# A five-part transformer block on one core: periods written out without loops, constants and statistics moved in the start, and an order of their own for each attention's first periods

## The chip, the cores and the metric

The kernel runs on one core of a Trainium2 chip. Its engines are TensorE (PE; its weight loads are PEld), VectorE (DVE), ScalarE (ACT), GpSimd (POOL) and SyncE (SP), which issues most DMAs. The metric is the time of one execution in microseconds (us): 991.41 before, the median of three runs (989.72 to 997.21). The profiled execution took 990.86, of which the span of its instructions is 989.1.

## What is computed

Eight batches of 56 tokens of width 128 (x) pass through four layers. L0 is a modulated cross attention with 16 heads of 8 onto a context of 1500 rows per batch; L1 is a one-head attention onto the same context with gated experts; L2 and L3 are blocks of self attention, cross attention onto the context with 16 heads, and an MLP. All in float32.

```python
xq = _ada_ln(x_q, t_vec, Wss_q, bss_q)           # L0
xkv = _ada_ln(x_kv, t_vec, Wss_kv, bss_kv)
q = (xq @ Wq + bq).reshape(B, Lq, nh, dh)
kv = (xkv @ Wkv + bkv).reshape(B, Lkv, 2, nh, dh)
scores = jnp.einsum('bqhd,bkhd->bhqk', q, k) / jnp.sqrt(jnp.float32(dh))
attn = jax.nn.softmax(scores, axis=-1)
...
q_c = _ln(x) @ W_qc + b_qc                       # L2, after its self attention
kv_c = _ln(context) @ W_kvc + b_kvc
...
kv = (context @ kv_w + kv_b).reshape(B, S, 2, H, HD)   # L3
```

## The kernel before

The three cross attentions with 16 heads (L0, L2, L3; class `Heads`) are most of the time. A context of 1500 rows is taken in three parts of 500 (j = 0 to 2), each of four pieces of 125 rows. For one batch the steps are, with the names used below:

- context work, by `deps`, `dpow`, `norm`, `hat` on POOL (L0 and L2 only): normalised rows `hat_sb`; T0 to T2: their transposes on PE (L511) and ACT's copies (L612, L616); K0 to K2: key products (L519), which ACT reads twice (L630) and POOL cuts into three bfloat16 parts (L753 to L760); V0 to V2: value products (L526), copied by ACT (L636). SP then stacks the key parts in `kstack` by 18 small DMAs (L364), six for each j. The queries are cut and stacked likewise in `qstack` (six DMAs, L355).
- maxima: 24 products M0.0 to M2.7 (L542, part j and pair of heads), each read by a DVE reduction (L675); then MTa and MTb, transposes of the maxima (L532), called MT below, whose result goes into `qstack` as a shift by DVE and ACT.
- scores S0 to S11 (L556, eight products each), exponentials E0 to E11 on ACT (L648), products with the values PV0 to PV5 (L568), then OT and OTT, which finish a batch.

All T, K, V, M, MT, OT and OTT share three PSUM banks (`ring_ps`). A bank is written again only when its last reader is done, and which bank a step has follows from the order written out (`ring_banks`). The period of batch n holds the scores of batch n, the maxima of batch n+1 and the context work of batch n+2, interleaved in an order written by hand (`pe`, `act`). `first_context` does the context work of batch 0 alone; the fill (period -1) has the maxima of batch 0 and the context work of batch 1, in an order `fill` on PE. `later_periods` (L187) emits the fill, period 0, a hardware loop of two turns with two periods each (periods 1 to 4), and periods 5 to 7 written out. In the loop, addresses and the values waited for are registers; `settle` adds a semaphore increment before some steps.

At the start, POOL clears one of two key stacks (L1466), and ACT clears the other and writes its two rows of ones (L1615) after the context work of batch 0. DVE takes the statistics of the eight contexts for L0 and L2 (L1686, L1690: 12 + 12 instructions each): batch 0 to 4 before the maxima, 5 to 7 in one block behind the fill (`after_first`). Twelve modulation products for the layers L2 and L3 (L1499, MODS_LATER) stand between K and V of batch 0. L1's attention is the class `Evidence`. `keep_busy` issues products whose result nobody reads. The own (self) attentions of L2 and L3 (class `Own`) run beside the context work of batch 0 of their cross attention: its V products stand just ahead of the own scores (L886).

## Time and profile before

| engine | busy us of 989.1 | share |
|---|---|---|
| PE | 868.6 | 88% |
| DVE | 606.3 | 61% |
| ACT | 507.4 | 51% |
| POOL | 361.6 | 37% |

The chain of work that ended last is 62% PE, 18% DVE, 9% issue, 5% ACT. The slices of 24.7 us show PE at 5, 7, 6, 6 tenths in the first 100 us and at 9 in the middle of each attention. In the rows below a group gives the busy time of the engines in a window with the number of instructions, the granted clock of PE (1.00 is 2.4 GHz, 0.50 is 1.2 GHz), the DMA engines' busy share and GB/s; or the instructions in order of time with what ended the idle time before them.

### The profile page before, as it was taken

The page shows a single profiled execution, that of the slowest core. Times are in us where ns is not written, and L with a number is a line of the kernel's source. Part 1 is how long each engine was busy: PE and PEld are TensorE (multiplying, and loading weights), DVE is VectorE, ACT ScalarE, POOL GpSimd, SP SyncE. Part 2 cuts the span into 40 slices and gives each one's busy share as a digit, 9 for nine tenths or more (in the row PEclk, how much of TensorE's full clock was granted, in tenths as well). Part 3 has the DMA queues.
Part 4 walks back from the last instruction along what each step waited for, and adds up shares of the span by engine and source line. Part 5 has one row for each costly group of instructions (what it writes and reads, how often), then busy time and mean ns, then how long its engine had stood idle before and what let it go on. Part 6 is the DMA issues. An engine that isn't in the chain of part 4 may idle for free.

```text
span 989.1 us, 24937 instructions
## 1 busy us (share of the span) xinstructions
PE 868.6 (88%) x9539; PEld 556.6 (56%) x9539; DVE 606.3 (61%) x1273; ACT 507.4 (51%) x754; POOL 361.6 (37%) x481
## 2 busy tenths in 40 slices
PE   5766999999898887778999999888787999999987
PEld 3434777776555434542777777554453466666653
DVE  7557777777332374555677777715464777777825
ACT  5565777775512213312777777441333466667551
POOL 6645666661000106147566664010313333333000
PEclk9677999999989999886999999999789799999999
DMA  9742444437326304307244443010334444443200
GB/s 264 201 112 77 126 127 125 124 95 257 109 114 188 94 0 132 99 16 197 74 122 132 124 125 98 19 63 1 87 94 125 120 126 126 126 124 95 64 2 9
DMA packets 76826, 106.67 MB, mean 108 GB/s; under 512 B 9371, under 2 KB 70427, under 8 KB 76481
## 3 DMA queue, kind: packets, MB, share of 16 engines
q1 hardware_dynamic: 75152, 102.65, 37.4%
q10 hardware_dynamic: 1584, 2.79, 1.0%
q8 instruction: 62, 1.02, 0.4%
q14 instruction: 28, 0.22, 0.1%
HBM read 41.56 MB, written 0.23 MB: 42 GB/s over the span
## 4 chain that ended last, share of the span: by engine, by line
PE 62%; DVE 18%; issue 9%; ACT 5%; POOL 3%; DMA 2%; SPq 1%; ACTq 0%; POOLq 0%; DVEq 0%
PE ring_ps L542 11%; PE oacc_ps L568 11%; PE score_ps L556 10%; PE ring_ps L526 7%; PE ring_ps L519 6%; DVE max_sb L675 4%; PE ring_ps L1174 4%; DVE tok L961 3%; PE ring_ps L532 2%; PE ring_ps L511 2%; PE oacc_ps L334 2%; ACT prob_sb L648 1%; POOL hat_sb L744 1%; DMA prob_sb<-ctx_T 1%; DVE bn_tmp L1686 1%
## 5 line engine op out<-in xcount | busy, mean ns | idle before, releaser
L675 DVE TENSOR_REDUCE max_sb<-ring_ps 128x1 f32<-128x500 f32 x576 | 364.0, 674 | 151.1 <-PE ring_ps L542 150.2
L648 ACT ACTIVATE prob_sb<-score_ps 125x896 f32<-125x896 f32 x288 | 255.1, 919 | 88.0 <-PE score_ps L556 87.0
L542 PE MATMUL ring_ps<-kstack,qstack 128*128 128x500 bf16 x576 | 201.1, 393 | 14.7 <-DVE max_sb L675 8.6
L753 POOL TENSOR_TENSOR key_sb<-key_sb,part_sb 128x500 f32<-128x500 f32 x72 | 81.8, 1136 | 236.8 <-ACT key_sb L630 236.8
L556 PEld LDWEIGHTS score_ps<-qstack,kstack 128*128 128x128 bf16 (+1 forms) x2304 | 138.3, 102 | 48.8 <-ACT prob_sb L648 13.1
L556 PE MATMUL score_ps<-qstack,kstack 128*128 128x112 bf16 (+3 forms) x2304 | 160.5, 214 | 5.9 <-ACT prob_sb L648 5.0
L568 PE MATMUL oacc_ps<-prob_sb,val_sb 125*32 125x168 f32 (+1 forms) x3456 | 139.5, 294 | 1.5 <-ACT prob_sb L648 1.4
L568 PEld LDWEIGHTS oacc_ps<-prob_sb,val_sb 125*32 125x32 f32 x3456 | 97.6, 109 | 48.8 <-issue 19.1
L542 PEld LDWEIGHTS ring_ps<-kstack,qstack 128*128 128x128 bf16 (+1 forms) x576 | 51.3, 98 | 87.7 <-issue 53.8
L744 POOL TENSOR_SCALAR hat_sb<-nat_sb,norm_now 125x128 f32<-125x128 f32 x192 | 87.2, 471 | 4.9 <-POOL norm_now L734 4.9
L760 POOL TENSOR_TENSOR part_sb<-key_sb,part_sb 128x500 bf16<-128x500 f32 x72 | 82.0, 1138 | 5.8
L1218 POOL TENSOR_TENSOR tok_rstd<-tok_var,minus_half 112x4 f32<-112x4 f32 x8 | 8.1, 1008 | 207.5 <-DVE tok_var L1232 207.5
L334 PE MATMUL oacc_ps<-ident,mean_mat 128*128 128x512 bf16 x272 | 72.7, 406 | 0.0
L636 ACT COPY val_sb<-ring_ps 125x384 f32<-125x384 f32 x72 | 34.6, 480 | 54.3 <-PE ring_ps L526 54.3
L519 PE MATMUL ring_ps<-ctxT_sb,w_sb 128*128 128x500 f32 x96 | 55.0, 666 | 5.8 <-ACT key_sb L630 5.8
L526 PE MATMUL ring_ps<-w_sb,ctxT_sb 128*125 128x128 f32 x384 | 55.6, 293 | 3.3 <-ACT val_sb L637 2.9
L630 ACT ACTIVATE part_sb<-ring_ps,vec_sb 128x500 bf16<-128x500 f32 x72 | 48.9, 679 | 17.8 <-PE ring_ps L519 14.2
L1252 ACT COPY qpart_sb<-prob_sb 64x448 bf16<-64x448 bf16 x30 | 16.9, 562 | 80.1 <-DVE prob_sb L1241 79.3
L526 PEld LDWEIGHTS ring_ps<-w_sb,ctxT_sb 128*125 128x125 f32 x384 | 52.9, 206 | 6.7 <-ACT val_sb L637 4.1
L1174 PE MATMUL ring_ps<-tok,w_sb 128*128 128x448 f32 x98 | 43.9, 584 | 10.5 <-DVE part_sb L1809 3.6
L511 PE MATMUL ring_ps<-ident,hat_sb 125*128 125x125 f32 x192 | 32.7, 299 | 23.2 <-DVE max_sb L675 8.6
L630 ACT ACTIVATE key_sb<-ring_ps,vec_sb 128x500 f32<-128x500 f32 x72 | 48.6, 675 | 0.0
(217 smaller groups left out, 993.6 us busy)
## 6 DMA issues: line engine op xcount, KB each, us to landing
kstack<-part_sb SPq DMA_DIRECT2D x432, 125.0 KB, 2.4
...
qstack<-qpart_sb SPq DMA_DIRECT2D x24, 224.0 KB, 3.6
...
```

The costliest lines, as they stand in the source:

```text
L334: pe.matmul(out.rearrange("p (a k) -> p a k", a=2), busy_lhs, busy_rhs, start=True, stop=True)
L519: last = pe.matmul(ps[:, 0:KB], self.wkey, self.context_T(u)[:, j * KB:(j + 1) * KB], start=True, stop=True)
L526: last = pe.matmul(ps[0:CK, c * D:(c + 1) * D], self.context_T(u)[:, k0:k0 + CK], self.wval, start=True, stop=True)
L542: last = pe.matmul(ps[:, 0:KB], queries(p, n, D), kstack[:, u, p, j * KB:(j + 1) * KB], start=True, stop=True)
L556: last = pe.matmul(score_ps[0:window(c), c % 2, p // 4, at:at + 2 * LQ], kstack[:, u, p, c * CK:c * CK + window(c)], queries(p, n), start= ...
L568: return pe.matmul(oacc_ps[tile * GW:(tile + 1) * GW, at:at + nh * LQ], val_sb[0:CK, u, c, g * GW:(g + 1) * GW], prob_sb[0:CK, c % PROBS, ...
L630: ins = act.activation(dst, src, ACT.Identity, bias=self.bkey)
L648: ins = act.activation(dst, score_ps[0:CK, c % 2, :, 0:HALF], ACT.Exp)
L675: ins = dve.tensor_reduce(max_sb[:, p, j:j + 1], ring_ps[:, self.bank[name], 0:KB], AX.X, ALU.max)
L744: ins = pool.tensor_scalar(hat_sb[:, c, :], nat_sb[0:CK, u, c, :], norm_now[:, 1, c:c + 1], norm_now[:, 0, c:c + 1], ALU.add, ALU.mult)
L760: ins = pool.tensor_tensor(part_sb[:, 2, cols], rest, part_sb[:, 1, cols], ALU.subtract)
L1174: last = pe.matmul(self.ps(name) if out is None else out, lhsT, rhs, start=(k == 0), stop=(k == len(pairs) - 1))
```

## The change

- The loops of `later_periods` and of SP's `sync_later` are written out; no registers are left in them. `settle` is gone.
- `fill` is gone. A table for each attention gives the place of the context steps on PE and ACT in its first periods (`EARLY_L0`, `EARLY_L2`, `EARLY_L3`: period -1 and 0, in L0 also 1); "K1:M0.2" puts K1 behind M0.2, "-" puts a step first. Banks follow from these orders, and `first_context` has banks of its own.
- POOL clears both key stacks at the beginning; ACT writes both pairs of rows of ones before its first copy. The queries' six DMAs go from ACT's queue to SP's, the first five ahead of the keys'.
- DVE takes the statistics of batches 1 to 4 before the maxima, and those of 5, 6 and 7 in periods 0, 1 and 2, one instruction behind each of the 24 maxima.
- The later modulations move into Evidence, on PE behind its first scores in the place of seven of ten filler products, on DVE behind the first maximum.

```diff
-def later_periods(body, eng, after_first=None):
+def later_periods(body):
 
     body(None, None, (0, 0, 0), (1, 1, 0))
-    if after_first:
-        after_first()
     body(None, (0, 0, 0), (1, 1, 0), (2, 0, 1))
-    with eng.Fori(0, (B - 4) // 2) as j:
-        body((2 * j, 0, j), (2 * j + 1, 1, j), (2 * j + 2, 0, j + 1), (2 * j + 3, 1, j + 1))
-        body((2 * j + 1, 1, j), (2 * j + 2, 0, j + 1), (2 * j + 3, 1, j + 1), (2 * j + 4, 0, j + 2))
+    for n in range(B - 4):
+        body(*((k, k % 2, k // 2) for k in range(n, n + 4)))
...
-                if modulated:
-                    fill = [*mm[0:8], "T0", *mm[8:10], "T1", *mm[10:12], "T2", "K0", *mm[12:16], "K1", *mm[16:20], "K2",
-                            *mm[20:24], "V0", "V1", "MTa", "MTb", "V2"]
-                else:
-                    fill = [*T3, "K0", "K1", "K2", "V0", "V1", *mm, "MTa", "MTb", "V2"]
-                self.fill = fill
...
+                def moved(eng, n):
+
+                    order, after = self.orders[eng], dict(x.split(":") for x in early[n][eng].split())
+                    fixed = [x for x in order if not context(eng, x) and (n >= 0 or lead(x) == 1)]
+                    return [y for x in ["-", *fixed] for y in ([x] if x != "-" else []) + [z for z in after if after[z] == x]]
+
+                self.early = {(eng, n): moved(eng, n) for n in early for eng in ("pe", "act")}
...
-                self.fill_bank = {**self.steady_bank, **ring_banks(fill)}
+                self.early_bank = {n: {**self.steady_bank, **ring_banks(self.early["pe", n])} for n in early}
+                self.first_bank = ring_banks([n for n in pe if context("pe", n)])
...
                 first = not nxt and far
-                filling = nxt and not cur and not prev
-                self.bank = self.fill_bank if filling else self.steady_bank
+                n = cur[0] if cur else -1 if nxt else B
+                self.bank = self.first_bank if first else self.early_bank.get(n, self.steady_bank)
...
-                for name in self.fill if filling and eng == "pe" else self.orders[eng]:
+                for name in self.early.get((eng, n), self.orders[eng]):
...
-                        settle(pe)
...
-                    keep_busy(pe, 2 if k else 10, ring_ps[:, 0, :])
+                    if k:
+                        keep_busy(pe, 2, ring_ps[:, 0, :])
+                    else:
+                        meanwhile()
+                        keep_busy(pe, 3, ring_ps[:, 0, :])
...
                 highest(0)
+                meanwhile()
                 inverse(0)
...
+        EARLY_L0 = {
+            -1: {"pe": "T0:M1.2 T1:M1.6 T2:M2.0 K0:M2.3 K1:M2.7 K2:M2.7 V0:MTb V1:MTb V2:MTb",
...
+            1: {"pe": "T0:S0 T1:M0.2 T2:M0.5 K0:M0.5 K1:S4 K2:M1.2 V0:M2.5 V1:M2.5 V2:MTb",
...
+            stack_queries(sp, queries_ready(d0), a0.qstacked, (0, 1))
             sp.wait_ge(keys_cleared, 1)
-            a0.sync_batch(sp, None, (0, 0, 0))
+            a0.sync_batch(sp, None, (0, 0, 0), lambda: stack_queries(sp, queries_ready(d0), a0.qstacked, (2,)))
...
-            sp.wait_ge(keys_cleared, 3)
+            sp.wait_ge(keys_cleared, 2)
...
-            pool.memset(kstack[:, 0, :, :].bitcast(F32), 0.0).then_inc(buffers_ready, 1)
-            pool.wait_ge(buffers_ready, 1)
+            for u in range(2):
+                pool.memset(kstack[:, u, :, :].bitcast(F32), 0.0).then_inc(buffers_ready, 1)
+            pool.wait_ge(buffers_ready, 2)
...
-            pe.wait_ge(loaded_wm, 16)
-            d.bank_free(pe, "mods1")
-            modulations(MODS_LATER, "mods1")
...
+            def later_modulations():
+                pe.wait_ge(d1.dve.sem, d1.dve.after("anchors"))
+                pe.wait_ge(loaded_wm, 16)
+                modulations(MODS_LATER, "mods1")
+
+            evi.tensor(pe, lambda eng: eng.wait_ge(d1.dve.sem, d1.dve.after("qk")), later_modulations)
...
-            act.wait_ge(buffers_ready, 1)
-            fill(key_stack(0)[SHIFT_ROW:SHIFT_ROW + 2, :], bf16_ones[:, :], 1.0).then_inc(keys_cleared, 1)
+            for u in range(2):
+                act.wait_ge(buffers_ready, u + 1)
+                fill(key_stack(u)[SHIFT_ROW:SHIFT_ROW + 2, :], bf16_ones[:, :], 1.0).then_inc(keys_cleared, 1)
             act.wait_ge(d.dve.sem, d.dve.after("scales0"))
             act.wait_ge(values_cleared, VALUES)
-            a0.first_context("act", act, 0)
             act.wait_ge(queries_cleared, 2)
-            for j in range(NJ):
-                a0.first_part("act", act, lambda name, j=j: name in (f"k0.{j}", f"K{j}"))
-                d.to_blocks(act, (j,))
-                stack_queries(act, queries_ready(d), a0.qstacked, (j,))
+            a0.first_part("act", act, lambda name: name in ("T0", "T1"), starts=True)
+            d.to_blocks(act, (0,))
+            a0.first_part("act", act, lambda name: name == "T2")
+            d.to_blocks(act, (1,))
+            a0.first_part("act", act, lambda name: name in ("k0.0", "K0"))
+            d.to_blocks(act, (2,))
+            a0.first_part("act", act, lambda name: name[0] in "kK" and name[-1] != "0")
             a0.first_context("act", act, 2)
-            fill(key_stack(1), mean_mat[:, 0:1], 0.0).then_inc(keys_cleared, 1)
-            act.wait_ge(keys_cleared, 2)
-            fill(key_stack(1)[SHIFT_ROW:SHIFT_ROW + 2, :], bf16_ones[:, :], 1.0).then_inc(keys_cleared, 1)
...
-            def statistics(n):
+            def statistics(n, steps=range(2 * NC)):
...
+            def later_statistics(name, cur):
+
+                if cur and cur[0] + STATS_FIRST < B and name in a0.mm:
+                    statistics(cur[0] + STATS_FIRST, (a0.mm.index(name),))
...
-            for n in (1, 2, 3):
+            for n in range(1, STATS_FIRST):
                 statistics(n)
-            modulations(MODS_LATER, SCALES_LATER, 1)
-            statistics(4)
-            a0.later("dve", dve, lambda: [statistics(n) for n in (5, 6, 7)])
+            a0.later("dve", dve, beside=later_statistics)
...
-            evi.vector(dve)
+            evi.vector(dve, lambda: modulations(MODS_LATER, SCALES_LATER, 1))
```

The order tables have 14 such strings in all; two are shown.

On PE from the key products of batch 0 into the fill stands before (L519 is K, L1499 a modulation product, L526 V, L542 M, L511 T):

```order
L519 MATMUL ring_ps<-ctxT_sb,w_sb 128x500 x3
L1499 MATMUL score_ps<-cond_silu,w_sb 128x8 x12
L526 MATMUL ring_ps<-w_sb,ctxT_sb 125x128 x12
L542 MATMUL ring_ps<-kstack,qstack 128x500 x8
L511 MATMUL ring_ps<-ident,hat_sb 128x125 x4
L542 MATMUL ring_ps<-kstack,qstack 128x500 x2
L511 MATMUL ring_ps<-ident,hat_sb 128x125 x4
L542 MATMUL ring_ps<-kstack,qstack 128x500 x2
L511 MATMUL ring_ps<-ident,hat_sb 128x125 x4
L519 MATMUL ring_ps<-ctxT_sb,w_sb 128x500
L542 MATMUL ring_ps<-kstack,qstack 128x500 x4
L519 MATMUL ring_ps<-ctxT_sb,w_sb 128x500
```

and now, with the same steps at other line numbers (L504 is K, L511 V, L527 M, L496 T):

```order
L504 MATMUL ring_ps<-ctxT_sb,w_sb 128x500 x3
L511 MATMUL ring_ps<-w_sb,ctxT_sb 125x128 x12
L527 MATMUL ring_ps<-kstack,qstack 128x500 x11
L496 MATMUL ring_ps<-ident,hat_sb 128x125 x4
L527 MATMUL ring_ps<-kstack,qstack 128x500 x4
L496 MATMUL ring_ps<-ident,hat_sb 128x125 x4
L527 MATMUL ring_ps<-kstack,qstack 128x500 x2
L496 MATMUL ring_ps<-ident,hat_sb 128x125 x4
L527 MATMUL ring_ps<-kstack,qstack 128x500 x3
L504 MATMUL ring_ps<-ctxT_sb,w_sb 128x500
L527 MATMUL ring_ps<-kstack,qstack 128x500 x4
L504 MATMUL ring_ps<-ctxT_sb,w_sb 128x500 x2
```

The modulation products are gone, and T and K come later among the M. Behind these rows stand before: four M, K2, four M, V0 and V1 of batch 1, MT, V2; now: MT and then V0 to V2.

On DVE from the fill's maxima into period 0 stands before (L1686 and L1690 are statistics, L675 the read of a maximum, L691 the shift):

```order
L675 TENSOR_REDUCE max_sb<-ring_ps 128x1 x24
L678 TENSOR_REDUCE max<-max_sb 128x8
L682 TENSOR_SCALAR maxb<-max 128x8
L685 CAST maxparts<-maxb 128x8
L687 SCALAR_TENSOR_TENSOR maxparts<-max,maxb 128x8
L691 CAST qstack<-ring_ps 2x4x112
L1686 BN_STATS bn_tmp<-w_sb 125x6 x12
L1690 BN_AGGR ctx_mv<-bn_tmp 125x2 x12
L1686 BN_STATS bn_tmp<-tok 125x6 x12
L1690 BN_AGGR ctx_mv<-bn_tmp 125x2 x12
L1686 BN_STATS bn_tmp<-w_sb 125x6 x12
L1690 BN_AGGR ctx_mv<-bn_tmp 125x2 x12
```

and now (L1710, L1712, L656, L672):

```order
L656 TENSOR_REDUCE max_sb<-ring_ps 128x1 x24
L659 TENSOR_REDUCE max<-max_sb 128x8
L663 TENSOR_SCALAR maxb<-max 128x8
L666 CAST maxparts<-maxb 128x8
L668 SCALAR_TENSOR_TENSOR maxparts<-max,maxb 128x8
L672 CAST qstack<-ring_ps 2x4x112
L656 TENSOR_REDUCE max_sb<-ring_ps 128x1
L1710 BN_STATS bn_tmp<-w_sb 125x6
L656 TENSOR_REDUCE max_sb<-ring_ps 128x1
L1710 BN_STATS bn_tmp<-w_sb 125x6
```

The block of three behind the fill's maxima has become single instructions between the maxima of a period.

On PE the head of the loop's first period (M0.0, OT, S0) is before

```order
L542 ISA
L542 MATMUL ring_ps<-kstack,qstack 128x500
L177 ISA x2
L586 MATMUL ring_ps<-ident,o_sb 56x128 x3
L589 MATMUL ring_ps<-fold_sb,o_sb 56x64 x2
L177 ISA x2
L556 ISA
L556 MATMUL score_ps<-qstack,kstack 128x112
L556 ISA
L556 MATMUL score_ps<-qstack,kstack 128x112
L556 ISA
L556 MATMUL score_ps<-qstack,kstack 128x112
```

and the head of period 1 now is, up to T0 of batch 3 and M0.1

```order
L527 MATMUL ring_ps<-kstack,qstack 128x500
L570 MATMUL ring_ps<-ident,o_sb 56x128 x3
L573 MATMUL ring_ps<-fold_sb,o_sb 56x64 x2
L541 MATMUL score_ps<-qstack,kstack 128x112 x8
L496 MATMUL ring_ps<-ident,hat_sb 128x125 x4
L527 MATMUL ring_ps<-kstack,qstack 128x500
```

Each of the eight products of S0 had an instruction ahead of it that sets a register for its address; now there is none.

## Rows read from the trace of the kernel before

**Rows 1.** Windows, cut from one MT's start to another's (columns: busy us and count)

```profile
105.91:205.90 99.99, 99.94 (x1293) 70.74 (x1289) 72.17 (x140) 74.23 (x112) 65.79 (x98) 1.00 0.46 124
205.90:230.41 24.51, 24.51 (x326) 17.52 (x322) 17.76 (x35) 18.48 (x28) 11.40 (x15) 1.00 0.32 87
495.10:594.02 98.92, 98.88 (x1293) 70.27 (x1290) 72.12 (x140) 72.59 (x112) 65.80 (x98) 1.00 0.46 126
594.02:618.36 24.34, 24.34 (x326) 17.48 (x323) 17.77 (x35) 17.98 (x28) 10.49 (x14) 1.00 0.36 96
801.06:898.60 97.54, 96.75 (x1244) 65.13 (x1241) 69.95 (x140) 65.28 (x100) 34.19 (x36) 1.00 0.45 127
898.60:922.01 23.41, 23.37 (x315) 15.96 (x311) 17.57 (x35) 16.23 (x25) 8.56 (x9) 1.00 0.37 101
```

**Rows 2.** Windows of the start, a clock drop, and L2's fill (columns as above)

```profile
0.00:100.00 100.00, 65.11 (x388) 41.48 (x389) 65.35 (x260) 54.27 (x62) 57.65 (x86) 0.80 0.61 164
20.00:45.00 25.00, 17.64 (x63) 13.06 (x62) 14.48 (x99) 9.75 (x19) 18.17 (x28) 0.61 0.98 246
278.00:280.00 2.00, 2.00 (x13) 2.00 (x13) 0.16 (x1) 0.00 (x0) 1.01 (x1) 0.58 0.03 8
460.00:472.00 12.00, 9.87 (x25) 2.95 (x25) 10.26 (x21) 0.21 (x1) 7.72 (x15) 0.50 0.44 119
```

**Rows 3.** Timeline of PE at the start (start, us, idle before in brackets)

```profile
32.15 5.13 PE L1499 MATMUL score_ps<-cond_silu,w_sb 128*128 128x8 f32 x24
...
44.59 1.91 PE L542 MATMUL ring_ps<-kstack,qstack 128*128 128x500 bf16 x4
...
56.74 1.06 PE L511 MATMUL ring_ps<-ident,hat_sb 125*128 125x125 f32 x4 [6.12 <-ACT ctxT_sb L612]
...
83.29 1.07 PE L511 MATMUL ring_ps<-ident,hat_sb 125*128 125x125 f32 x4 [8.42 <-DVE max_sb L675]
```

**Rows 4.** Timeline of ACT at the start

```profile
18.41 0.77 ACT L612 ACTIVATE ctxT_sb<-ring_ps,mod_sb 128x500 f32<-128x500 f32 x1 [4.85 <-PE ring_ps L511]
...
45.51 5.20 ACT L1615 ACTIVATE kstack<-mean_mat 128x6000 f32<-128x6000 f32 x1
```

**Rows 5.** Timeline of DVE, the last of three statistics

```profile
79.23 2.42 DVE L1686 BATCH_NORM_STATS2 bn_tmp<-w_sb 125x6 f32<-125x128 f32 x12
81.68 0.90 DVE L1690 BATCH_NORM_AGGREGATE ctx_mv<-bn_tmp 125x2 f32<-125x6 f32 x12
```

**Rows 6.** Timeline of PE, S0 of L3: first loop period, then period 5

```profile
802.88 1.18 PE L556 MATMUL score_ps<-qstack,kstack 128*128 x8
...
900.52 0.55 PE L556 MATMUL score_ps<-qstack,kstack 128*128 128x112 bf16 x8
```

**Rows 7.** Timeline of POOL at the start

```profile
1.24 5.10 POOL L1466 MEMSET kstack<- 128x6000 f32 x1
...
14.93 7.00 POOL L744 TENSOR_SCALAR hat_sb<-nat_sb,norm_now 125x128 f32<-125x128 f32 x12 [0.25 <-POOL norm_now L734]
...
39.95 5.16 POOL L744 TENSOR_SCALAR hat_sb<-nat_sb,norm_now 125x128 f32<-125x128 f32 x12 [0.24 <-POOL norm_now L734]
```

**Rows 8.** DMA issues from 20 to 48 us (count, KB each, us to landing)

```profile
kstack<-part_sb SPq DMA_DIRECT2D x18, 125.0 KB, 4.1
qstack<-qpart_sb ACTq DMA_DIRECT2D x6, 224.0 KB, 4.9
```

**Rows 9.** Timelines of L2: PE (V1, S0), SP (queries), DVE (maxima)

```profile
402.35 2.07 PE L526 MATMUL ring_ps<-w_sb,ctxT_sb 128*125 128x128 f32 x8 [0.74 <-ACT val_sb L637]
...
442.48 3.79 SPq L355 DMA_DIRECT2D qstack<-qpart_sb  x6
...
454.84 14.22 DVE L675 TENSOR_REDUCE max_sb<-ring_ps 128x1 f32<-128x500 f32 x24 [11.51 <-PE ring_ps L542]
...
473.25 0.56 PE L556 MATMUL score_ps<-qstack,kstack 128*128 128x112 bf16 x8
```

**Rows 10.** Timeline of PE in Evidence, first transposes

```profile
294.12 1.57 PE L1045 MATMUL ring_ps<-ident,key_sb 128*125 128x128 f32 x12 [1.27 <-ACT key_sb L1074]
```

More of the change, by code:

```diff
@@ L793, in load_T, with sync_batch @@
                 sp.dma_start(self.context_T(u), ctx_T[n]).then_inc(self.loaded[u], 16)
-            def sync_batch(self, sp, before, this):
+            def sync_batch(self, sp, before, this, beside=None):
                 n, u, half = this
@@ L811, in sync_batch @@
                         stack_keys(sp, part_sb, part, u, slice(j * KB, (j + 1) * KB), self.stacked[u][j])
+                        if beside and j == 0 and part == 0:
+                            beside()
             def sync_load(self, sp):
@@ L1335, in project, with mods_out @@
             return product
+        def mods_out(step):
+            return d0.ps(step) if step == "mods0" else score_ps[:, 1, 1, :]
         def own_pe(d, pe, l, x_ready):
```

86 lines of the change are left out of this document (40 added, 46 removed), and 12 rows, old and new, of tables (EARLY_L0, EARLY_L2, EARLY_L3).

## The prediction

> **What bounds the kernel now.** I read the windows of the periods first. From one MT (transposes of the maxima) to the next TensorE (PE) is busy all the time at full clock: 24.51 of 24.51 us in period 5 of L0 [rows 1]. Such a period is bound by PE. In the first 100 us it is busy 65.1 us only, at a granted clock of 0.80, and from 20 to 45 us the DMA engines are 0.98 busy at 246 GB/s [rows 2]. So the start is bound by something else, and the timelines there name it. The first M (product for the maxima) starts only at 44.59, behind the later modulations (5.13) and the V products in PE's order [rows 3]. Then ScalarE (ACT) runs two fills of the second key stack, the first at 45.51 for 5.20, the other behind it, and PE waits 6.12 for ACT's copy of a transpose [rows 3, 4]. Then VectorE (DVE) runs the statistics of three contexts, up to 82.5, and PE waits 8.42 for a ring bank that DVE must read first [rows 3, 5].
>
> Then the pace of the middle, again by windows cut at the starts of MT: the loop's four periods take 99.99 us in L0, 98.92 in L2 and 97.54 in L3, so 25.00, 24.73 and 24.39 each; period 5, the same work written out, takes 24.51, 24.34 and 23.41 [rows 1]. The difference sits where each of the eight products of S0 has a register instruction ahead of it in the loop: S0 lasts 1.18 in a loop period of L3 and 0.55 written out [rows 6].
>
> **The start of L0.** All against the profiled execution: span 989.1, time 990.86; the median of the runs, 991.41, is 0.5 above.
> POOL's second clearing of key rows (the first took 5.10 from 1.24 [rows 7]) ends at 11.44, and the power that makes the deviations, at 10.95 before, comes 0.5 late with all behind it. ACT's second row of ones (5.2) goes behind the first, to 18.8; the first T copy stood at 18.41 after a wait of 4.85 [rows 4], which hides the fill. Without that cover it costs 5.2. The two key fills at 45.5 are gone from ACT.
> POOL's first hats took 7.00, beside DVE's casts on SBUF, later ones 5.16 [rows 7]. At that ratio the second clearing takes 6.9 and the start is 2.3 late instead of 0.5. I take 0.5, since DVE mostly runs statistics there, and keep 2.3 as the bound. A rule speaks for the bound: the Trainium skill (GPSIMD Engine Reference, section Key points) says that GpSimd shares its SBUF interfaces with VectorE and contends with some of its instructions. By it the sum would be 1.8 higher; the trace agrees with it on the hats.
> With the modulations gone, K2 and the V products not waiting for a bank, ACT is done with the keys at about 30 and PE with V at about 33. M0.0 needs the stacked queries and the first third of the stacked keys. In 20 to 45 us DMA moved 246 x 25 = 6.15 MB [rows 2], of which queries are 1.38, keys 2.30 [rows 8] and the last context 0.77, so 1.7 MB of loads lie ahead of them; queries and a third of the keys are in after (1.70 + 1.38 + 0.77) / 0.246 = 15.7 us, at 35.7. That the queries now go through SP's queue, behind the context loads, is in this sum. DVE does four statistics of 3.4 in a row behind its query split and is free at 35.2. So M begins at about 35.5, 9.1 earlier.
> 24 maxima take DVE 14.2 [rows 9], to 50.1. T0 to T2 of batch 1 sit at M1.2 to M2.0, about 42 to 47, and POOL's hats can be ready from 40.5 to 44: no wait. K1 and K2 come behind M2.7, MT at about 52, then all three V, so S0 at 56.5. Bounds: 55 at full clock, 60 if PE stays at half clock as it did in L2's fill (0.50 in 460 to 472 [rows 2]).
> Period 0: in L2, which has no statistics, S0 to MT is 495.10 - 473.25 = 21.85 [rows 1, 9]. The statistics become 24 pieces in each of three periods, 2.42 + 0.90 = 3.3 us [rows 5]. DVE is busy 18.0 in a loop period [rows 1] and stays under PE with 21.3, but the first half is tight: I take 0.7 for each of the three, between 0 (all in gaps) and 3.3 (all paid). MT behind period 0 comes at 56.5 + 21.85 + 0.7 + 0.5 (clearing) = 79.5 instead of 105.91: **-26.4**.
> Period 1: POOL cuts batch 2's keys until about 79.3, needs 2.8 for the deviations and 1.7 for a first hat, to 83.8, while PE reaches T0 behind S0 at about 82.2: **+1.6** (0 to 4). The statistics of periods 1 and 2 add 1.4, and T1 and T2 asked for later give back 0.7: **+0.7**.
>
> **The loops.** Four periods each at the written-out pace: 99.99 - 98.04 = 1.95 in L0, 98.92 - 97.36 = 1.56 in L2, 97.54 - 93.64 = 3.90 in L3 [rows 1]: **-7.4**. Registers of the other engines go too, but hide behind PE.
>
> **L2.** In the own attention V1 and V2 now have a bank free: two waits of 0.74 for ACT go [rows 9], ahead of the first own scores: **-1.5** (0 if something else is late there). In the fill M starts at 450 instead of 454.4, since the last of six query DMAs is issued by 446.3 [rows 9] and the products ahead of it are fewer; but K1, K2 and V stand between the M. PE at half clock then needs 24 x 0.42 + 9.2 = 19.3, to 469.4, and DVE was done at 469.1: no gain. At full clock DVE's 14.2 plus 2 ends at 466.3. I take 1.2. V2 no longer stands between MT and S0: 0.8. **-2.0** (-5 to +0.5).
> **L3.** One such wait goes in the own part, **-0.7**. In the fill the first M waits for the query DMAs, which nothing moves; V products moved into it and V2 taken out cancel: 0 (-2 to +1.5).
>
> **The later modulations** now run beside Evidence: 5.13 at half clock [rows 3], so 2.6 at full, in the place of seven filler products. PE stood there filling from 290.5, and waited 1.27 for ACT's exponential until 294.12 [rows 10]: 290.5 + 2.6 + 0.7 for three fillers = 293.8, hidden, and DVE's two small steps too. What can come is the clock: it fell to 0.58 in 278 to 280 [rows 2], where PE ran the 8-column anchor products, and these have that form. At half clock for some 6 us, 3 are lost, and U0 behind them releases DMAs of the chain. I take **+1.0** (0 to 3.3).
>
> Sum: -26.4 + 1.6 + 0.7 - 7.4 - 1.5 - 2.0 - 0.7 + 1.0 = -34.7. 990.86 - 34.7 = **956.2**.
>
> **Rivals.**
> 1. The start gives a good part back: statistics fully paid (3 x 3.3 less the 2.1 counted, +7.8), fill at half clock (+3.5), clearing late (+1.8), hats late (+2.4), together 15.5: 971.7. For it: PE and DVE are both near full in those periods. Against: three ring banks absorb pieces of 0.2.
> 2. DMA bounds the start, and M0.0 comes no earlier than 44. Then PE still saves the 6.12 and the 8.42: 990.86 - 14.5 - 7.4 - 3.2 = 965.8. For it: the 0.98. Against: the bytes above.
> 3. The edit does not do what it says: each wait is followed by the next one (hat, stack, bank). The loops alone: 983.5, within 1%.
> 4. Slower: PE's stream is longer, and fetching it stalls in the twelve periods newly written out. It decides from 34.7 / 12 = 2.9 us each; at 4 us 990.86 - 34.7 + 48 = 1004.2. Against it: period 5 is such code and runs with PE busy throughout [rows 1].
> The Trainium skill (Runtime: NRT & Kernel Launch, Instruction fetch mechanics) says that the sequencer streams straight code ahead and that a taken branch breaks this; by it rival 4 has next to no chance, and the trace agrees on straight code. The 0.03 below does not rest on it.
>
> **How the numbers follow.** Forecast (944 to 966) 0.77; rivals 1 and 2 (966 to 981) 0.15; rival 3 0.05; rival 4 0.03. Range 944 to 972: the low end is the sum with hats and statistics free (-4), the L2 fill at full clock (-3), no clock loss (-1) and 4 more of PE's idle time in the first 100 us; the high end takes in rival 1 whole. One per cent, 9.9 us, is about what a measurement here can tell from no change. Faster 0.92, same 0.05, slower 0.03.
>
> **What would show it.** After: first M at 35 to 36, MT at 52 and 79.5; no ACT fill behind 19; periods 2 to 4 at 24.5, 24.3 and 23.4; small pieces on DVE between the maxima of periods 0 to 2, and no PE wait over 1 us there; own scores of L2 1.5 closer to V0; clock 1.00 beside Evidence. A first M behind 40, PE waiting over 2 us for DVE in one of the periods 0 to 2, or written-out periods over 25 would make it wrong.

## The result and the profile after

The changed kernel takes 963.46 us (median of four runs, 960.46 to 968.04) against 990.98 before in the same comparison: a ratio of 0.971 with the interval 0.966 to 0.976, so 27.5 us faster where 34.7 had been forecast. The profiled execution took 962.78, with a span of 961.0; before the span was 989.1. What follows sets the marks of this execution against those of the profiled execution before; a mark is the start of a step on PE.

The page's slices of 24 us (tenths of busy time, and of the granted clock) show the start filled up: PE reads 6 5 8 9 in the first four slices, 5 7 6 6 before:

```profile
PE   6589999998997897877999999888686899999986
...
PEclk9699999999899998878999999999887799999999
```

Windows of the changed kernel: from S0 to the MT behind period 0 of L0, its period 1, periods 2 to 4, period 5 (compare [rows 1]); then S0 to MT and periods 1 to 4 of L2; then M0.0 to the fill's MT, S0 to MT, and periods 1 to 4 of L3. Columns as in [rows 1]: start and end, length, then the busy time and count of PE, of its weight loads, of DVE, ACT and POOL, then the granted clock, the DMA share and GB/s.

```profile
62.16:86.08 23.92, 22.45 (x299) 15.04 (x298) 18.95 (x52) 18.05 (x27) 19.15 (x28) 1.00 0.52 139
86.08:112.00 25.92, 25.09 (x322) 17.34 (x322) 20.90 (x59) 18.33 (x28) 21.37 (x35) 1.00 0.52 138
112.00:185.53 73.53, 73.53 (x967) 52.55 (x968) 56.85 (x129) 55.18 (x84) 48.87 (x73) 1.00 0.46 125
185.53:209.95 24.42, 24.42 (x326) 17.53 (x322) 17.77 (x35) 18.39 (x28) 11.13 (x14) 1.00 0.36 96
446.00:468.85 22.85, 22.84 (x298) 16.51 (x299) 15.91 (x28) 16.88 (x25) 14.49 (x20) 0.93 0.32 87
468.85:566.34 97.49, 97.49 (x1292) 69.92 (x1288) 72.16 (x140) 72.16 (x112) 65.91 (x98) 1.00 0.47 127
...
732.92:751.31 18.39, 13.35 (x49) 5.68 (x49) 15.18 (x28) 1.94 (x6) 4.49 (x5) 0.78 0.83 185
753.93:777.87 23.94, 23.53 (x287) 15.16 (x287) 15.71 (x28) 15.29 (x22) 8.56 (x9) 0.88 0.31 82
777.87:870.82 92.95, 92.83 (x1244) 63.87 (x1240) 70.31 (x140) 64.80 (x100) 34.24 (x36) 1.00 0.47 134
```

The written-out periods run at the pace of period 5, as forecast. What was not forecast stands in the last three rows: the fill of L3 takes 18.39 (15.4 before), and period 0 of L3 runs at a clock of 0.88, for 23.94 (21.2 before).

The account of the whole, from one mark of PE to the next (us, negative is faster):

| stretch | forecast | measured |
|---|---|---|
| start of L0 to the MT behind period 0 | -26.4 | -19.8 |
| period 1 of L0 (hats, pieces, loop) | +1.8 | +0.9 |
| rest of L0 | -1.5 | -1.5 |
| L0's last MT to the own scores of L2 | -0.5 | -6.2 |
| fill and period 0 of L2 | -2.0 | +0.4 |
| periods 1 to 4 of L2 | -1.6 | -1.4 |
| L2's last MT to the own scores of L3 | -0.7 | -2.0 |
| own scores to the MT behind period 0 of L3 | 0 | +6.5 |
| periods 1 to 5 of L3 | -3.9 | -4.8 |
| behind L3 | 0 | -0.2 |
| sum | -34.7 | -28.1 |

The start, on PE (start, us, idle before in brackets): M0.0, MT and S0.

```profile
38.12 6.14 PE L527 MATMUL ring_ps<-kstack,qstack 128*128 128x500 bf16 x11 [7.29 <-DMA kstack<-part_sb]
...
57.92 1.03 PE L517 MATMUL ring_ps<-ident,maxparts 128*2 128x128 f32 x8 [1.95 <-DVE maxparts L668]
...
62.16 0.56 PE L541 MATMUL score_ps<-qstack,kstack 128*128 128x112 bf16 x8
```

M0.0 waits for a transfer, and comes 2.6 behind the 35.5 of the forecast; MT is 5.9 behind its 52, S0 5.7 behind its 56.5. The two waits of [rows 3, 4, 5], for ACT's copy and for the block of statistics, are gone. On DVE two of the five waits between the maxima, and the two small steps ahead of MT:

```profile
45.85 2.44 DVE L656 TENSOR_REDUCE max_sb<-ring_ps 128x1 f32<-128x500 f32 x4 [0.49 <-PE ring_ps L527]
48.78 1.27 DVE L656 TENSOR_REDUCE max_sb<-ring_ps 128x1 f32<-128x500 f32 x2 [0.50 <-PE ring_ps L527]
...
55.58 1.13 DVE L663 TENSOR_SCALAR maxb<-max 128x8 bf16<-128x8 f32 x1
56.74 1.05 DVE L666 CAST maxparts<-maxb 128x8 f32<-128x8 bf16 x1
```

### The profile page after: what moved, and what is told of

It reads as the page before. It is cut to its first block, busy times and chain, and to the rows that moved or that the text cites. A ratio compares the mean times of both kernels' runs of the same rounds, so it can differ in the third digit from the quotient of the medians.

```text
span 961.0 us, 22829 instructions
## 1 busy us (share of the span) xinstructions
PE 848.7 (88%) x9532; PEld 546.9 (57%) x9532; DVE 607.5 (63%) x1273; ACT 499.9 (52%) x753; POOL 366.4 (38%) x482
## 3 DMA queue, kind: packets, MB, share of 16 engines
q10 hardware_dynamic: 720, 1.41, 0.5%
## 4 chain that ended last, share of the span: by engine, by line
PE 62%; DVE 16%; issue 8%; POOL 5%; ACT 4%; DMA 3%; SPq 1%; POOLq 0%; DVEq 0%; ACTq 0%
PE ring_ps L527 13%; PE oacc_ps L553 11%; PE score_ps L541 10%; PE ring_ps L511 6%; PE ring_ps L504 6%; DVE max_sb L656 4%; PE ring_ps L1162 4%; DVE tok L944 3%; PE ring_ps L517 2%; PE ring_ps L496 2%; PE oacc_ps L320 2%; ACT prob_sb L630 1%; POOL hat_sb L722 1%; DMA prob_sb<-ctx_T 1%; POOL kstack L1482 1%
## 5 line engine op out<-in xcount | busy, mean ns | idle before, releaser
L656 DVE TENSOR_REDUCE max_sb<-ring_ps 128x1 f32<-128x500 f32 x576 | 366.6, 674 | 136.8 <-PE ring_ps L527 134.8
L527 PE MATMUL ring_ps<-kstack,qstack 128*128 128x500 bf16 x576 | 198.9, 390 | 28.3 <-DVE max_sb L656 9.0
L541 PE MATMUL score_ps<-qstack,kstack 128*128 128x112 bf16 (+1 forms) x2304 | 158.2, 215 | 6.9 <-ACT prob_sb L630 5.0
L527 PEld LDWEIGHTS ring_ps<-kstack,qstack 128*128 128x128 bf16 x576 | 50.9, 98 | 96.5 <-issue 50.1
L511 PE MATMUL ring_ps<-w_sb,ctxT_sb 128*125 128x128 f32 x384 | 49.7, 275 | 3.1 <-ACT key_sb L612 1.8
L504 PE MATMUL ring_ps<-ctxT_sb,w_sb 128*128 128x500 f32 x96 | 51.2, 627 | 0.8 <-ACT key_sb L612 0.3
L511 PEld LDWEIGHTS ring_ps<-w_sb,ctxT_sb 128*125 128x125 f32 x384 | 47.1, 188 | 6.5 <-ACT key_sb L612 2.8
L320 PEld LDWEIGHTS oacc_ps<-ident,mean_mat 128*128 128x128 bf16 x272 | 28.5, 108 | 37.0 <-issue 18.3
```

The source lines that it names most:

```text
L320: pe.matmul(out.rearrange("p (a k) -> p a k", a=2), busy_lhs, busy_rhs, start=True, stop=True)
L504: last = pe.matmul(ps[:, 0:KB], self.wkey, self.context_T(u)[:, j * KB:(j + 1) * KB], start=True, stop=True)
L511: last = pe.matmul(ps[0:CK, c * D:(c + 1) * D], self.context_T(u)[:, k0:k0 + CK], self.wval, start=True, stop=True)
L527: last = pe.matmul(ps[:, 0:KB], queries(p, n, D), kstack[:, u, p, j * KB:(j + 1) * KB], start=True, stop=True)
L541: last = pe.matmul(score_ps[0:window(c), c % 2, p // 4, at:at + 2 * LQ], kstack[:, u, p, c * CK:c * CK + window(c)], queries(p, n), start= ...
L656: ins = dve.tensor_reduce(max_sb[:, p, j:j + 1], ring_ps[:, self.bank[name], 0:KB], AX.X, ALU.max)
```

## Experiments

Each kernel was profiled once, beside timed runs of the kernel before; the marks are read from its trace. A time marked "once" is that of a single execution; one of those is no measure of a difference of a few us, and there the marks carry the reading.

### The loops alone

```diff
# the kernel before
-    with eng.Fori(0, (B - 4) // 2) as j:
-        body((2 * j, 0, j), ...)
+    for n in range(B - 4):
+        body(*((k, k % 2, k // 2) for k in range(n, n + 4)))
# the same in sync_later, and no increment in settle
```

> The kernel before with only its loops written out (periods 1 to 4 of each attention on every engine, SP's too, and the settle increments gone); nothing else is moved. Theory 1 (the pace of a written-out period is all that the loops are worth, as predicted): the four periods from MT to MT take 98.0 in L0, 97.4 in L2, 93.6 in L3 or a little less, time 983.5 (983 to 984.5), all other marks as in the kernel before, Evidence and the own attention of L2 among them. Theory 2 (the 2.0 us that the changed kernel gained inside Evidence and the 2.0 more than forecast in L2's own attention come with the straight code): the same stretches are 2 shorter here too, time 979.5. Theory 3 (straight code stalls somewhere): a period over 25.

978.74 median (975.02 to 983.88), a ratio of 0.987 (0.982 to 0.993). Periods 1 to 4 of L0, L2 and L3:

```profile
104.70:202.66 97.96, 97.96 (x1292) 70.09 (x1288) 72.28 (x140) 73.63 (x112) 65.96 (x98) 1.00 0.47 126
485.93:583.54 97.61, 97.61 (x1292) 69.87 (x1289) 72.28 (x140) 72.22 (x112) 66.15 (x98) 1.00 0.47 128
789.91:882.88 92.97, 92.86 (x1245) 63.83 (x1242) 70.32 (x140) 64.83 (x100) 34.30 (x36) 1.00 0.47 134
```

Against [rows 1] they gain 2.0, 1.3 and 4.6, together 7.9 where 7.4 was forecast; period 5 of L3, which was written out before, gains another 0.2 (23.41 to 23.23) now that settle's increments are gone. S0 lasts 0.56 to 0.57 in these periods. In the loop it took 1.00 to 1.26 in L3 [rows 6], but only 0.57 to 0.80 in L0 and L2: S0 holds about half of L3's gain of 1.14 a period and a quarter of the 0.50 and 0.33 of the other two. Where in the period the rest is gained is not shown. No period is over 25, so theory 3 is out. But the median fell by 12.6, and from L0's last MT to the own scores of L2 this kernel took 149.4 instead of 154.6, with the same instructions. Theory 2 had said something like that; the next run asks whether that stretch varies by itself.

### The kernel before, again

> The kernel before, once more, unchanged. From the last MT of L0 to the first own scores of L2 the kernel before took 154.64 in its profile; the four profiles of kernels with written-out loops show 148.41 to 149.97 there, though Evidence and the own attention are the same work in the kernel with only its loops written out. Theory 1 (that stretch varies from execution to execution with the clock's dips and DMA waits): 149 to 153 here. Theory 2 (loops or settle cost something behind the attentions too): 154 to 155 again, and the periods 25.0, 24.7 and 24.4 again.

988.2, once. The stretch took 152.4, as theory 1 has it, and the periods of the loop were 25.0, 24.8 and 24.4 again (means). The twelve kernels with written-out periods, the changed one among them, took 147.5 to 152.2 there, 149.8 in the mean; the kernel before 154.6 and 152.4. So the stretch varies by 2 between two executions of one kernel and by 4 to 5 over kernels that have nearly the same work in it, and of the 6.2 in the table 3.7 are left by the means, 1 to 2 of them for the two V waits (below). Whether straight code, or settle's going, gains the rest stays open: two profiles of the kernel before are too few to tell.

### The old fills of L2 and L3

```diff
# the changed kernel
-            -1: {"pe": "K0:- K1:- K2:- V0:M0.5 V1:M1.2 V2:M1.3",           # L3
+            -1: {"pe": "K0:- K1:- K2:- V0:- V1:- V2:MTb",
# and the like in L2: T, K, V0, V1 first, V2 behind MT
```

> The changed kernel with the fill (period -1) of L2 and of L3 in the old order: K and V0, V1 ahead of the first M, V2 behind MT; period 0 keeps its new order. The changed kernel took 18.4 from the first M to MT in L3 where the kernel before took 15.4, and PE stood idle for 6.69 ahead of the first M. Theory 1 (V products between the maxima starve DVE, and the idle PE stays at half clock into period 0): M to MT in L3 falls to 15.4, MT to S0 rises from 2.6 to 3.4, S0 to the MT behind period 0 falls from 23.9 to about 21.5, so L3 ends 4.5 earlier; in L2 S0 to MT falls from 22.85 to 21.85, its fill stays within 1. Theory 2 (the new order of period 0 itself is slower): the fills change by 2 at most and both periods 0 stay at 22.85 and 23.9, L3 ends 2 earlier.

956.59, once. M to MT and S0 to MT of L3:

```profile
731.44:746.84 15.40, 12.37 (x25) 2.37 (x26) 14.73 (x28) 0.00 (x0) 4.88 (x6) 0.56 0.78 179
...
750.20:771.41 21.21, 20.98 (x288) 13.85 (x287) 15.70 (x28) 15.70 (x24) 8.55 (x9) 0.99 0.45 129
```

Theory 1 holds to 0.3 in each of the three stretches: the fill 3.0 shorter, MT to S0 0.7 longer, period 0 2.7 shorter; L3 ends 5.0 earlier by them, where 4.5 was expected. In L2 M to MT is 15.43 and S0 to MT 21.86, with MT to S0 at 3.4, but M0.0 comes 4.2 later behind the own scores, so that the MT behind period 0 is only 1.1 earlier behind them. In the changed kernel DVE, the pace of a fill, stood idle 1.41 when V0 came between the maxima and took 2.07 at half clock:

```profile
735.07 2.50 DVE L656 TENSOR_REDUCE max_sb<-ring_ps 128x1 f32<-128x500 f32 x4 [0.17 <-PE ring_ps L527]
738.98 3.02 DVE L656 TENSOR_REDUCE max_sb<-ring_ps 128x1 f32<-128x500 f32 x5 [1.41 <-PE ring_ps L527]
```

while ahead of the maxima PE stands idle for the queries' transfers anyway, and V0 and V1 are free. The clock of the changed kernel from MT on, four us each:

```profile
751.31:755.31 4.00, 3.24 (x18) 2.17 (x19) 0.61 (x1) 0.96 (x2) 0.00 (x0) 0.50 0.00 0
755.31:759.31 4.00, 4.00 (x13) 1.73 (x13) 1.36 (x2) 2.56 (x4) 1.03 (x1) 0.50 0.00 0
```

and of this one, with V2 behind MT:

```profile
746.84:750.84 4.00, 4.00 (x25) 3.34 (x26) 0.61 (x1) 0.91 (x3) 0.00 (x0) 0.55 0.00 0
750.84:754.84 4.00, 3.80 (x33) 2.08 (x31) 2.04 (x3) 3.95 (x8) 1.49 (x2) 1.00 0.57 192
```

With V2 behind MT PE was busy for all of the first four us, and the clock was back at 1.00 behind them; with V2 moved away it took eight, and the first 5.4 us of period 0 ran at 1.2 GHz. V2 is all that differs on PE between MT and S0; the run moved V0 and V1 along with it, and none moved V2 alone.

### The steady order in periods 0 and 1

```diff
# the changed kernel: EARLY_L0[0], EARLY_L0[1], EARLY_L2[0] and EARLY_L3[0] are left out
```

> The changed kernel with the steady order of steps in period 0 (and 1) of L0, L2 and L3; only the fills keep their new orders. Theory 1 (the clock, not the order, makes period 0 of L2 and L3 long): S0 to MT stays at 22.85 in L2 and 23.9 in L3 (plus or minus 0.5), and in L0 period 0, whose T then stand ahead of POOL's hats, grows from 23.9 by up to 6 and period 1 by 2. Theory 2 (the order of period 0 is slower than the steady one): L2 and L3 fall to 21.9 and 21.2 here. If the new orders in L0 are worth nothing, its period 0 stays at 23.9.

967.6, once. S0 to MT is 22.45 in L2 and 23.62 in L3: their long period 0 is not the order's, as theory 1 says. In L0 it grew to 28.72, as theory 1 says too, but period 1, which was to grow by 2, fell to 24.60:

```profile
61.92:90.64 28.72, 23.45 (x299) 16.33 (x298) 18.95 (x52) 17.93 (x27) 23.81 (x37) 0.94 0.46 126
90.64:115.24 24.60, 24.60 (x326) 17.46 (x322) 20.78 (x59) 18.39 (x28) 16.62 (x26) 1.00 0.47 127
```

The order of period 0 that puts T behind POOL's hats is worth 4.8; 1.3 of it is given back in period 1, where POOL is behind in its turn. PE busy 24.60 of 24.60 beside the pieces of a context's statistics on DVE also says what those cost: 0.1 against the 24.46 of a period without.

### Loads behind the first keys

```diff
-            for n in range(2, 7):
+            for n in range(2, 5):
                 load_context(sp, stats_buffer(n), n, stats_loaded[n])
...
             a0.sync_batch(sp, None, (0, 0, 0), ...)
+            for n in range(5, 7):
+                load_context(sp, stats_buffer(n), n, stats_loaded[n])
```

> The changed kernel with the loads of contexts 5 and 6 (0.77 MB each) issued behind the stacking of the first keys instead of ahead of it; their statistics are taken in periods 0 and 1 only. In the changed kernel M0.0 came at 38.12, forecast was 35.5, and from 30 to 38 us DMA was 1.11 busy at 240 GB/s. Theory 1 (transfers bound the first M): it comes earlier by up to 2 x 0.77 / 0.24 = 6, cut off by DVE, whose fourth statistics end at 36.5, so at 33 to 36.5, and MT of the fill 1.6 to 2 earlier (56.2). Theory 2 (POOL's cut of the keys or the issue on SP's queue bounds it): M0.0 stays at 37.5 to 38.1.

961.29, once. PE at M0.0:

```profile
32.64 0.81 PE L527 MATMUL ring_ps<-kstack,qstack 128*128 128x500 bf16 x3 [1.30 <-DMA kstack<-part_sb]
36.43 4.70 PE L527 MATMUL ring_ps<-kstack,qstack 128*128 128x500 bf16 x8 [2.98 <-DVE max_sb L656]
```

1.54 MB fewer ahead of the keys brought M0.0 forward by 5.5, so transfers bound it. That is a little more than theory 1 had, and MT came at 54.46 where 56.2 was expected, 3.5 earlier than in the changed kernel: DVE's fourth statistics take 3 of the gain back, as the wait of 2.98 shows.

### Joined, with fewer statistics and earlier T and K

```diff
# the old fills and the late loads, all of ACT's key copies ahead of the shift, and
-        STATS_FIRST = 5
+        STATS_FIRST = 4
-            -1: {"pe": "T0:M1.2 T1:M1.6 T2:M2.0 K0:M2.3 K1:M2.7 K2:M2.7 V0:MTb ...   # L0
+            -1: {"pe": "T0:M1.2 T1:M1.5 T2:M1.7 K0:M2.0 K1:M2.2 K2:M2.5 V0:MTb ...
```

> The changed kernel with the old fills of L2 and L3, the loads of contexts 5 and 6 behind the first keys, three contexts' statistics ahead of the maxima instead of four (STATS_FIRST = 4: batch 4 in period 0 and so on), and T1, T2, K0 to K2 of L0's fill earlier (behind M1.5, M1.7, M2.0, M2.2, M2.5) with all of ACT's key copies ahead of the shift. Theory 1 (DVE's fourth statistics were what M waited for once the transfers were out of its way, and POOL's cut of the keys is what makes DVE's maxb and part0 1.1 long instead of 0.17): maxima from 33.2, MT of the fill at 51 to 52 instead of 57.92, POOL's cut ends before maxb or else maxb stays slow; MT behind period 0 at 79 to 80.5 instead of 86.08; with the 6.9 of L3 and 1.1 of L2, 949 by the profile. Theory 2 (hats and bank waits take the place): MT of period 0 at 83 or later, 953.

957.73 median (955.00 to 959.46). Maxima began at 33.19, but MT came at 54.81 and MT behind period 0 at 85.09: theory 2, though the time is above the 953 that it named. POOL's hats of batch 1 came at 38 to 43 as before (its cut of the first keys ends at 35.2, as it does with four statistics and the late loads), so T0 could start at 39.77 only, and DVE waited 1.60 there, and 1.18 more behind the K. POOL's cut then ran beside the end of the maxima. DVE, and POOL in the same stretch:

```profile
53.16 0.43 DVE L663 TENSOR_SCALAR maxb<-max 128x8 bf16<-128x8 f32 x1
53.63 1.05 DVE L666 CAST maxparts<-maxb 128x8 f32<-128x8 bf16 x1
```

```profile
52.44 1.13 POOL L737 TENSOR_TENSOR part_sb<-key_sb,part_sb 128x500 bf16<-128x500 f32 x1
53.53 1.13 POOL L731 TENSOR_TENSOR key_sb<-key_sb,part_sb 128x500 f32<-128x500 f32 x1
```

Each of the two small steps ends within 0.03 of the end of a POOL instruction. In the changed kernel they took 1.13 and 1.05 in the same way, from 55.58; in L2, where POOL makes no keys then, 0.17 each. S0 then stood 6.36 behind MT instead of 4.24, at a clock of 0.73.

### The statistics in a block again

```diff
-            a0.later("dve", dve, beside=later_statistics)
+            a0.later("dve", dve, beside=block)       # 5, 6, 7 behind the fill's shift
```

> The changed kernel with the statistics of 5, 6 and 7 in one block behind the fill's shift again, not spread. Theory 1 (as predicted, PE waits for the block): DVE is busy with it for 10.2 from 59.2, PE waits 4 to 7 for a ring bank in period 0, MT behind it comes at 90 to 93 instead of 86.08, and periods 1 and 2 get 0.7 shorter each (spread pieces cost about 0.7 a period). Theory 2 (pieces cost all their time, 3.3 a period): period 0 grows by 4 and periods 1 and 2 fall by 1 and more. Theory 3 (the statistics were not the bound of period 0, POOL's hats are): MT stays within 1 of 86.08.

971.14, once. On PE:

```profile
70.26 1.01 PE L527 MATMUL ring_ps<-kstack,qstack 128*128 128x500 bf16 x2 [5.68 <-DVE max_sb L656]
```

S0 to MT grew from 23.92 to 31.19. MT came at 93.64, 7.6 later, a little past the range of theory 1. But periods 1 and 2 fell by 0.19 and 0.12 only, not 0.7 each: the pieces are nearly free, and theory 2 is out; so is theory 3.

### The modulations back at the start

```diff
# PE: between K and V of batch 0; DVE: ahead of the fourth statistics; ten fillers in Evidence
-            modulations(MODS_LATER, "mods1")          # in Evidence
+            modulations(MODS_LATER, "mods1")          # behind first_context("pe", pe, 1)
```

> The changed kernel with the later modulations back between K and V of batch 0, and ten fillers in Evidence. Theory 1 (transfers bound M0.0 of the changed kernel, so the modulations' going away was not what brought it forward): M0.0 stays at 38.1 to 38.6 and the time within 1 of the changed kernel. Theory 2 (as predicted, M0.0 comes earlier as they go): M0.0 at 40 to 44, DVE's fourth statistics later too. In Evidence, theory 1: from its first scores to the first transposes 6.3 in either; a clock cost would show as a shorter stretch here.

967.21, once; but the marks that the edit can reach moved little. M0.0 came at 39.26 (38.12 to 39.11 in the five kernels with this start), MT at 58.36 (57.60 to 58.21), L0's last MT at 233.44 (232.63 to 233.07 in three of them). So their place at the start is worth under 1 once transfers bound M0.0. The single time is 3.8 above the changed kernel's median, not within 1 as theory 1 has it, and most of that stands behind L0, in stretches that vary between the kernels: 151.4 instead of 148.4 up to the own scores of L2, and 22.17 instead of 20.52 in L2's fill. In Evidence first scores to first transposes took 6.3 here, in the changed kernel and before, and the clock was 1.00 beside the modulations in the changed kernel: no clock cost.

### The clearing back on ACT

```diff
-            for u in range(2):
-                pool.memset(kstack[:, u, :, :].bitcast(F32), 0.0).then_inc(buffers_ready, 1)
+            pool.memset(kstack[:, 0, :, :].bitcast(F32), 0.0).then_inc(buffers_ready, 1)
...
             a0.first_context("act", act, 2)
+            fill(key_stack(1), mean_mat[:, 0:1], 0.0) ...
+            fill(key_stack(1)[SHIFT_ROW:SHIFT_ROW + 2, :], bf16_ones[:, :], 1.0) ...
```

> The changed kernel with the clearing as in the kernel before: POOL clears one key stack, ACT clears the other and writes its ones (2 x 5.2) behind the V copies of batch 0. In the changed kernel ACT is idle from 31.5 to 45.4 and its first copy comes at 19.97 instead of 18.41. Theory 1 (once V and the queries no longer hold ACT back, the fills lie in that idle time): first copy at 18.4 to 18.7, fills from 31 to 41.5, no wait of PE for ACT, MT of the fill at 57.9 or up to 1 earlier. Theory 2 (the fills are on the path as they were before, where PE waited 6.12 for ACT): MT of the fill 3 to 6 later, at 61 to 64.

963.19, once. ACT, and PE at M0.0:

```profile
31.77 5.21 ACT L1633 ACTIVATE kstack<-mean_mat 128x6000 f32<-128x6000 f32 x1
37.02 5.20 ACT L1633 ACTIVATE kstack<-bf_ones 2x6000 f32<-2x6000 f32 x1
47.12 0.77 ACT L594 ACTIVATE ctxT_sb<-ring_ps,mod_sb 128x500 f32<-128x500 f32 x1 [4.90 <-PE ring_ps L496]
```

```profile
39.81 6.14 PE L527 MATMUL ring_ps<-kstack,qstack 128*128 128x500 bf16 x11 [8.60 <-DMA kstack<-part_sb]
```

The fills lie in ACT's idle time with 4.9 to spare, and the first copy came at 18.38, as theory 1 says. PE's wait of 6.12 for ACT did not come back: what took the fills off the path is that V and the queries no longer hold ACT back. But MT came at 59.30, behind a later M0.0, and so between the theories and 1.1 behind the latest of the others. S0 stood 5.59 behind it instead of 4.24:

```profile
59.30:64.89 5.59, 5.51 (x33) 4.75 (x34) 0.61 (x1) 2.95 (x8) 4.04 (x5) 0.69 0.69 195
```

L0 ended 2.8 later than in the changed kernel. Two kernels that leave the clearing on POOL show such a clock there too (0.73 in the joined one, 0.71 in the one with the old fills and the late loads), so it need not be the clearing's; one execution does not tell. Moving the clearing is thus worth between nothing and 2.8, and not the 6.12.

### Fillers ahead of the first M of L3

```diff
+                if eng == "pe" and n == -1 and not first and not self.hat:
+                    keep_busy(engine, 16)
```

> The changed kernel with 16 filler products on PE ahead of the first M of L3's fill, where it stood idle for 6.69; the V products stay among the maxima. Theory 1 (V products among the maxima are dear because PE is at half clock there): M to MT in L3 falls from 18.4 to 16.5, S0 to MT from 23.9 to 21.2. Theory 2 (they are dear in themselves, by the ring banks that they take from the maxima, and the clock falls again while DVE paces the fill): M to MT 17.5 or more, S0 to MT 23 or more. The first M itself moves by 0 to 1.

962.5, once. They stood ahead of the K products, at full clock, and left PE idle for 2.92 behind K instead of 6.69. M to MT stayed at 18.39 and S0 to MT at 23.97, the numbers of theory 2. V0 took 2.07 all the same:

```profile
732.60 0.99 PE L529 MATMUL ring_ps<-kstack,qstack 128*128 128x500 bf16 x2 [2.92 <-issue]
...
736.13 2.07 PE L513 MATMUL ring_ps<-w_sb,nat_sb 128*125 128x128 f32 x8
```

So the fillers did not bring full speed to V0, and the run leaves open whether V among the maxima is dear by the half clock or by the ring banks that it takes.

### The old fills and the late loads

```diff
# the two edits above together, no other
```

> The changed kernel with the old fills of L2 and L3 and the loads of contexts 5 and 6 behind the first keys; all else as in the changed kernel. Theory 1 (what the single profiles showed adds up): L0 3.5 shorter, L3 6.9, L2 1.1: 952 from the median of 963.5; reckoned from the joined kernel (957.7, with L0's last MT at 232.22 where the late loads alone gave 229.47) 955. Theory 2 (an earlier attention's gain is lost in the stretches between attentions): 957 to 960.

956.98 median (956.02 to 958.66), a ratio of 0.964 (0.962 to 0.967): between the two theories, and no lower than the one time of the old fills alone (956.59). L2 and L3 kept their gains. In L0 MT came at 55.22, and S0 only 5.86 behind it, where the same instructions took 4.23 in the run with the late loads alone, at a clock of 0.71 instead of 1.00. With MT 0.8 later that made L0 end at 231.87 instead of 229.47: 2.4 between two executions of the same code.

### A filler behind every M of a fill

```diff
# the kernel of the last run, and in run():
                         emit(name, batches[self.lead(name)], prev, cur, nxt)
+                        if eng == "pe" and n == -1 and not first and name in self.mm:
+                            keep_busy(engine, 1)
```

> The changed kernel with the old fills of L2 and L3 and the late loads (as in e9_best, 956.98 median), and one filler product (512 columns, 0.21 at full clock, 0.43 at half) behind each of the 24 M of every fill. The sequence that DVE paces (0.59 an M) then holds 0.43 of PE's time an M at full clock, 0.85 at half. Theory 1 (PE's idle time in the fill is what lets its clock fall to 0.50 there and stay there into the steps behind MT): the clock is 1.00 in most of the fill, MT lasts 1.03 instead of 1.87, MT to S0 falls from 3.4 to 2.3 in L2 and L3, first M to MT is 15.4 to 16.7; the time 953 to 957. Theory 2 (the clock stays at half whatever stands between the M): M to MT 20 or more in L2 and L3, the time 967 or more.

953.37 median (949.95 to 953.95), a ratio of 0.960 (0.955 to 0.966); its slowest run is 2.1 below the fastest of the kernel without the fillers, and the medians differ by 3.6. The two profiles are no measure of that difference: the one is of its kernel's fastest execution, the other of its kernel's slowest. M to MT and MT to S0 of L2 without the fillers, then with them, then of L3 with them:

```profile
429.07:444.47 15.40, 12.24 (x25) 2.42 (x25) 14.73 (x28) 0.41 (x2) 13.59 (x22) 0.59 0.65 177
444.47:448.25 3.78, 3.78 (x17) 2.84 (x18) 0.61 (x1) 0.70 (x2) 0.00 (x0) 0.50 0.00 0
```

```profile
421.93:437.34 15.41, 13.23 (x49) 3.09 (x50) 14.75 (x28) 0.48 (x2) 12.54 (x21) 1.00 0.60 165
437.34:439.29 1.95, 1.95 (x17) 1.65 (x18) 0.61 (x1) 0.53 (x2) 0.00 (x0) 1.00 0.00 0
725.16:740.56 15.40, 13.18 (x48) 3.09 (x48) 14.74 (x28) 0.00 (x0) 4.56 (x5) 1.00 0.80 171
740.56:743.81 3.25, 3.25 (x16) 2.67 (x17) 0.61 (x1) 0.52 (x1) 0.00 (x0) 0.52 0.00 0
```

The fillers cost nothing in these fills, and the clock is 1.00 through both. In L2 it stays so into S0, which comes 1.8 earlier behind MT than without. In L3 it is at 0.52 again behind MT, and 0.1 is gained. PE waits for DVE ahead of MT in both, 1.77 in L2 and 1.78 in L3, so that wait alone does not say why; the cause stays open. In L0's fill the clock was 0.80 (0.77 without), and M0.0 to MT took 20.99, where the two kernels without fillers and with the late loads took 21.82 and 22.28. So about 1.8 of the 3.6 has its place in L2, some 1 may stand in L0, and the rest is not placed. This is the fastest of the kernels.

## Why the prediction was right, and where it was off

The direction and the range held, and 27.5 came where 34.7 was forecast. The terms are further apart than the sum: the start gave 6.6 less, L2's fill and period 0 2.4 less and L3's 6.5 less, while 5.7 came from L0's last MT to the own scores of L2 that no step foresaw, part of it the variation of that stretch. That the sum came within 7 is to that extent luck. By its own steps:

- **The loops** (-7.4): 7.9 alone. Right in size, and in place only in part: S0 with its registers holds about half of the difference in L3 and a quarter in L0 and L2. No period stalled, so rival 4 is out.
- **First M at 35.5**: 38.12. The step said that queries and a third of the keys are in at 35.7 by the bytes; their transfers are the bound, as it said, but bytes by the mean rate came 2.4 short, and the late loads show that each context ahead of them costs 2.7. Rival 2 named this bound; its 44 was too late.
- **Maxima in 14.2, MT at 52**: this step failed most. From M0.0 to MT the sum had 16.5, the trace 19.8. Left out were the waits of DVE where T and K stand between the maxima (1.9 in five waits; the mean clock from M0.0 to MT was 0.70, and what the half clock has in them is not told apart) and the small steps beside POOL's cut (1.8). POOL against DVE was weighed, but for the hats and at the wrong place.
- **Period 0 at 21.85 + 0.7 + 0.5**: S0 to MT 23.92. The spread statistics cost 0.1 a period, not 0.7, and were worth 7.3 against the block; the new order of its steps, behind POOL's hats, is worth 4.8 against the steady one.
- **Period 1, +1.6 and +0.7**: hats cost 1.3, pieces 0.1. The mechanism was right, the pieces too dear.
- **The clearing (0.5) and ACT's fills**: POOL began the power at 11.44, as forecast, but ACT's first copy came at 19.97, 1.6 later than before; M0.0, which waits for a transfer, hid it. The forecast gave the end of PE's wait for ACT to the fills' going. With them put back the wait stays away: it went with the earlier V and queries.
- **The modulations** (9.1 of the earlier M partly theirs; +1.0 in Evidence): under 1 at the start, 0 in Evidence.
- **L2's own V waits** (-1.5): gone, as in the profile; from the first own products to the own scores 15.2 fell to 11.2. The kernels with both waits took 15.2, 12.4 (the kernel before, again) and 13.0 (the loops alone), so 1 to 2 is theirs. The rest of the 6.2 is the stretch that varies between executions.
- **L2's fill (-2.0)**: +0.4. M0.0 came 4.8 earlier behind the own scores (forecast 4.4), and the 0.8 for V2 is there, but M0.0 to MT grew from 15.5 to 20.5, past the whole gain, where 1.2 of it was to be left, and period 0 took 1.0 more at a clock of 0.93.
- **L3's (0)**: +6.5. The step that failed is "V products moved into it and V2 taken out cancel". V0 and V1 had been free in PE's wait for the queries; with V among the maxima the fill took 3.0 more; and without V2 behind MT the clock came back only in period 0, for 2.7 there less the 0.7 of V2. Of the 6.5, 5.0 came back with the old order; 1.5 lies ahead of M0.0, in a stretch that took 41.0 to 43.1 over all the kernels.

The Trainium skill (SBUF — State Buffer, SBUF: two separate sides) says that a GpSimd instruction and a VectorE instruction in a two-port mode (or one with two SBUF inputs, against a GpSimd one that reads SBUF) take a shared pair of ports as a lock for the whole instruction. The trace agrees with a lock: 1.05 to 1.13 instead of 0.17, ending with POOL's instruction, for TENSOR_SCALAR and CAST, and not for TENSOR_REDUCE, which took 0.18 beside the same cut (at 52.95 in the joined kernel). In which mode the small steps ran no run here shows.
